# A comparison of two ways to transpose, put behind the last product of a Mamba-style layer and its feed-forward net

## The reference, cut to what matters

```python
x = x + _L0_attn_ref(_layernorm(x), ...)   # state-space layer: 128 heads of 64, 8 groups, gated, normed
x = x + _L0_ffn_ref(_layernorm(x), ...)    # gated feed-forward net, 1376 wide, with rank-16 additions
return x
```

```python
h1 = _lora_linear(x, w1, lora_A1, lora_B1)
h3 = _lora_linear(x, w3, lora_A3, lora_B3)
g = jax.nn.silu(h1) * h3
return _lora_linear(g, w2, lora_A2, lora_B2)
```

## Time and profile before

| | before |
|---|---|
| median of 3 executions | 1797.84 us (1797.22 to 1798.07) |
| the profiled execution, its own time | 1797.56 us |
| its span, first to last instruction | 1795.7 us |
| TensorE busy | 1762.8 us, 98% |
| VectorE busy | 1208.1 us, 67% |
| mean granted TensorE clock | 0.999 |

### The profile page before, as it was taken

The page is one execution under the profiler, slowest core; times in us unless marked ns, Lnnn a source line. Parts: engine busy times, 40 slices in busy tenths (PEclk is TensorE's granted clock), DMA queues, the critical chain, the costliest instruction groups (busy, mean ns, idle before and its releaser), DMA issues.

```text
span 1795.7 us, 27437 instructions
## 1 busy us (share of the span) xinstructions
PE 1762.8 (98%) x9826; PEld 1418.2 (79%) x9826; DVE 1208.1 (67%) x2081; ACT 1152.7 (64%) x2192; POOL 1079.3 (60%) x1011
## 2 busy tenths in 40 slices
PE   7999999999999999999999999999999999999999
PEld 5778887878788887888788878888788888787777
DVE  7796677757685768676876777576857697653313
ACT  5877577766766677667675776667666777552411
POOL 4475657566666567665756576666666575663510
PEclk9999999999999999999999999999999999999999
DMA  4643435333544443433534353345434443433201
GB/s 151 182 119 113 119 111 168 86 121 115 157 119 115 117 145 108 120 106 116 165 108 119 101 161 107 110 124 156 118 110 113 135 122 111 117 88 113 79 10 47
DMA packets 121878, 211.01 MB, mean 118 GB/s; under 512 B 24240, under 2 KB 28976, under 8 KB 121744
## 3 DMA queue, kind: packets, MB, share of 16 engines
q1 hardware_dynamic: 121744, 209.26, 40.3%
HBM read 204.48 MB, written 4.72 MB: 117 GB/s over the span
## 4 chain that ended last, share of the span: by engine, by line
PE 80%; DVE 8%; POOL 4%; issue 3%; DMA 3%; ACT 1%; SPq 0%; POOLq 0%; DVEq 0%; ACTq 0%
PE bank L1581 13%; PE bank L1583 13%; PE bank L1582 13%; PE bank L1692 6%; PE bank L1693 6%; PE bank L1694 6%; PE bank L1650 6%; PE bank L1680 5%; PE bank L1663 4%; DVE ow_l L1299 3%; DMA decay<-cum_scratch 3%; POOL gT_l L681 2%; PE bank L1626 2%; POOL decay L663 2%; PE bank L1901 1%
## 5 line engine op out<-in xcount | busy, mean ns | idle before, releaser
L657 POOL TENSOR_TENSOR w_l<-w_raw,w_h 128x512 fp32r<-128x512 f32 x288 | 380.2, 1324 | 465.2 <-ACT w_h L831 464.9
L1581 PE MATMUL bank<-x_h,w_h 128*128 128x512 f32 (+1 forms) x1328 | 532.9, 401 | 5.7 <-DVE bcT L1293 2.9
L1583 PE MATMUL bank<-x_h,w_l 128*128 128x512 f32 (+1 forms) x1328 | 519.1, 391 | 0.0
L1582 PE MATMUL bank<-x_l,w_h 128*128 128x512 f32 (+1 forms) x1328 | 518.1, 390 | 0.0
L1293 DVE SCALAR_TENSOR_TENSOR x_ch<-bank,par,x_ch 128x511 f32<-128x511 f32 (+2 forms) x384 | 287.5, 749 | 102.7 <-ACT x_ch L849 93.6
L884 ACT ACTIVATE decay<-decay,cols 128x128 f32<-128x128 f32 x1024 | 316.3, 391 | 0.8
L1581 PEld LDWEIGHTS bank<-x_h,w_h 128*128 128x128 f32 (+1 forms) x1328 | 249.3, 188 | 66.0 <-issue 8.7
L1583 PEld LDWEIGHTS bank<-x_h,w_l 128*128 128x128 f32 (+1 forms) x1328 | 248.8, 187 | 55.0
L1582 PEld LDWEIGHTS bank<-x_l,w_h 128*128 128x128 f32 (+1 forms) x1328 | 249.6, 188 | 48.0
L849 ACT ACTIVATE x_ch<-bank,par 128x512 f32<-128x512 f32 x128 | 99.4, 776 | 219.1 <-PE bank L1583 219.0
L1322 DVE TENSOR_TENSOR decay<-decay,bank 128x512 f32<-128x512 f32 x256 | 172.3, 682 | 92.9 <-ACT decay L884 92.7
(11 more groups left out here) (147 smaller groups left out, 2575.4 us busy)
## 6 DMA issues: line engine op xcount, KB each, us to landing
w_raw<-in_wp SPq DMA_DIRECT2D x288, 256.0 KB, 2.9
decay<-cum_scratch SPq DMA_DIRECT2D x256, 256.0 KB, 3.9
ec<-ecum_scratch SPq DMA_DIRECT2D x96, 256.0 KB, 6.4
ow_raw<-in_ow SPq DMA_DIRECT2D x64, 256.0 KB, 4.9
w_raw<-in_w SPq DMA_DIRECT2D x48, 256.0 KB, 2.7
acc<-in_x SPq DMA_DIRECT2D x8, 256.0 KB, 5.4
out<-acc SPq DMA_DIRECT2D x8, 256.0 KB, 2.0
cols<-cols_scratch SPq DMA_DIRECT2D x16, 96.0 KB, 2.8
```

The costliest lines, as they stand in the source:

```text
L657: pool.tensor_tensor(w_l[:, s, :], w_raw[:, s, :], w_h[:, s, :].bitcast(F32), ALU.subtract).then_inc(wl_ready, 1)
L1581: pe.matmul(dst, wh, xh, start=(k == 0), stop=False)
L1582: pe.matmul(dst, wh, xl, start=False, stop=False)
L1583: last = pe.matmul(dst, wl, xh, start=False, stop=(k == len(terms) - 1 and not more))
```

## The change

`acc` gets a second name, `acc_r`, of type fp32r at the same place in SBUF, and bank 1 gets the name `other` in that type. Two semaphores are new. TensorE gets eight transposes behind its last product: it waits until the results of chunks 0 and 1 are out of banks 0 and 1, then turns the four 128x128 tiles of chunk 7 of `acc` with fp32 operands into bank 0, and the same tiles with fp32r operands into bank 1, the two kinds in turn. VectorE waits for them after the addition of chunk 6, copies bank 0 to `xn`, subtracts bank 1, adds chunk 7's product to `acc` as before, and then adds 1e12 times the difference; only this last step increments `result_ready` for chunk 7.

```diff
-        acc = sb("acc", [P, CHUNKS, HID])
+        with nc.sbuf_tensor("acc", [P, CHUNKS, HID], F32) as acc:
+            pass
+        acc_r = sb("acc_r", [P, CHUNKS, HID], F32R)
...
+        other = bank[1].bitcast(F32R)
...
+        turned = sem("turned")
+        differ = sem("differ")
...
-            for c in range(CHUNKS):
+            for c in range(CHUNKS - 1):
                 dve.wait_ge(f_psum, c + 1)
                 dve.tensor_tensor(acc[:, c, :], bank[c][:, :], acc[:, c, :], ALU.add).then_inc(result_ready, 1)
+            dve.wait_ge(turned, 1)
+            dve.tensor_copy(xn[:, 0, :], bank[0][:, :]).then_inc(differ, 1)
+            dve.wait_ge(differ, 1)
+            dve.tensor_tensor(xn[:, 1, :], xn[:, 0, :], bank[1][:, :], ALU.subtract).then_inc(differ, 1)
+            dve.wait_ge(f_psum, CHUNKS)
+            dve.tensor_tensor(acc[:, CHUNKS - 1, :], bank[CHUNKS - 1][:, :], acc[:, CHUNKS - 1, :], ALU.add).then_inc(differ, 1)
+            dve.wait_ge(differ, 3)
+            dve.scalar_tensor_tensor(out=acc[:, CHUNKS - 1, :], in0=xn[:, 1, :], scalar=1e12, in1=acc[:, CHUNKS - 1, :],
+                                     op0=ALU.mult, op1=ALU.add).then_inc(result_ready, 1)
...
+            pe.wait_ge(result_ready, 2)
+            for q in range(KT):
+                pe.transpose(bank[0][:, tok(q)], acc[:, CHUNKS - 1, tok(q)], ident[:, :])
+                last = pe.transpose(other[:, tok(q)], acc_r[:, CHUNKS - 1, tok(q)], ident_r[:, :])
+            last.then_inc(turned, 1)
```

## The result

| | before | changed |
|---|---|---|
| median of 13 executions each | 1798.07 us (1797.10 to 1799.44) | 1801.74 us (1799.99 to 1802.11) |
| ratio to before, 95% interval | | 1.0018 (1.0009 to 1.0026) |
| span of the profiled execution | 1795.7 us | 1799.9 us |
| its own time | 1797.56 us | 1801.75 us |

The change costs 0.18%, about 3.2 us, with an interval from 1.6 to 4.7. That is inside the 0.2% that was called the same, as forecast, and near its edge: the interval reaches beyond it. The measured median lies 1.0 us above the predicted 1800.7 and inside the range.

A forecast was written before the change was run, and what follows sets the result against it. The prediction took the serial line from TensorE's last product to the last byte stored as the bound. TensorE's 0.77 plus VectorE's 2.05 gave 2.82 us on the 1797.84 us median, forecast 1800.7 us, range 1799.5 to 1802.3.

The forecast's parts named there:

- What bounds the end: Behind TensorE's last product, everything stands in series to the last byte stored; every added step costs its full length.
- VectorE's part: Copy, subtraction, addition and last operation at the end: 2.74 us where the addition alone took 0.69, 2.05 us added.
- TensorE's part: Eight transposes behind the last product, first start 0.23 us after it, each kind at its own step: 0.77 us added.
- The store: Chunk 7's store at the end: same size and place, 2.4 us from issue to end, only later.
- The sum: Steps added behind the last product: 0.77 + 2.05 = 2.82 us.
- The total: Time of the whole changed kernel: 1800.7 us, from the 1797.84 us median of three runs plus the added steps.
- this sign of being wrong: Ahead of the tail: the forecast would be wrong if TensorE's last product itself moved by more than 0.5 us.
- Rival 1: Between fp32 and fp32r transposes: alternation holds TensorE up, 1.2 us more, 1801.9 us (1803.0 with weight loads exposed); 17%.
- Rival 2: Under the eight transposes: the clock falls to 1.2 GHz, 0.8 us over forecast, 1801.5 us; 4%.
- Rival 3: Nearly nothing seen: steps overlap more, 1800.3 us, or an unrelated build difference; 3% for a gain over 3.6 us.

The follow-up runs named there:

- The parts alone: Two kernels: the changed kernel without VectorE's copy, subtraction and addition of the difference, 1799.56 us; the changed kernel without the eight transposes, 1800.56 us.
- the second: Profile of the changed kernel measured once more with no edit: 1801.57 us against 1798.43 for the kernel before, ratio 1.0015.
- the run with VectorE's part alone: The changed kernel without its eight transposes, the copy waiting for chunk 7's last product: 1800.56 us against 1798.43 for the kernel before, ratio 1.0012.

## Why the prediction was right

- What bounds the end: right. The parts alone (0.72 and 2.07 us behind the last product) add up to the whole (2.76 and 2.85). Moved out of the line, VectorE's part vanishes and TensorE's (0.78) stays, as TensorE is busy throughout.
- TensorE's part: forecast 0.77, measured 0.69. The start 0.23 behind the last product was right. The steps taken from each kind's own group were a little too long, since a pair in turn takes 0.17 and not 0.19.
- VectorE's part: forecast 2.05, measured 2.05. Each row read for it held: 0.69 for the copy, 0.72 from start to start with a wait, 0.60 to 0.61 without, 0.69 for the last operation.
- The store: forecast unchanged, 2.4 us; it was 2.43 in the first profile and 2.5 in the second, the same within the rounding of the span.
- The sum: forecast 2.82, and 2.76 in the first profile (2.85 in the second). The measured ratios, 1.0018 and 1.0015, are 3.2 and 2.7 us, with intervals that hold the sum.
- The total, 1800.7 against 1801.74: the total was 1.0 us off, and the steps behind the last product account for none of it. Of it 0.2 is the base: the median of three runs, 1797.84, stood for a kernel whose medians in the later sets were 1798.07, 1798.43 and 1798.98. The other 0.8 is what the medians of the first comparison differ by (3.67) beyond the forecast sum (2.82). It lies inside the interval (1.6 to 4.7), so it is not shown to be anything but spread. Everything ahead of the last product was forecast to stay "as it was", and by more than 0.5 us it did not; but neither does it in the unchanged kernel. So this sign of being wrong came up (1.44 us), and it was badly chosen: it asked of one profile what one program doesn't keep from one execution to the next. Over the profiles with the same stream ahead of the last product, that product starts anywhere from 1792.06 to 1794.26. The forecast had put the spread into its range by the 0.85 us between three runs, and it is over 3 us between 33. That the result counts as the same is in part luck: the interval reaches from 0.09% to 0.26%, across the line at 0.2%.
- Rival 1 (kinds in turn hold TensorE up): out; in turn is the faster order. Rival 2 (clock): out, also over 5.5 us. Rival 3 (a difference that has nothing to do with the steps): the medians are 3.67 and 3.14 us apart against the 2.8 of the tail, 0.3 to 0.9 more. The intervals hold 2.8, so such a difference is neither shown nor excluded.

The part ahead varies by 2 us in three places that the traces show: when the step between products gets shorter near the start, how long TensorE waits for GpSimd at 464 us, and what happens around the stretch of low clock near 1536 us (in the run with VectorE's part alone it lasted longer). What decides these from one execution to the next stays open.

## What to carry to other kernels

Work added behind the last product costs its full length, however short the engines' busy time makes it look. The same work where its engine sits idle is free: here that held for VectorE's part, not for TensorE's, and the banks for the comparison were free 11 us earlier. To price it, count from the last shared instruction in both traces and not from the start of the span: here the tail repeats to within 0.1 us while everything ahead of it moves by 2. On VectorE, a wait for its own last result costs 0.12 to 0.13 us for a 128x512 operation on fp32, so independent operations are best put between dependent ones.

## What was not expected of the hardware

- A transpose of a 128x128 tile took 0.109 us from start to start with fp32 operands and 0.084 with fp32r ones, but a pair in turn 0.174 rather than 0.193, over 28 pairs. The row of an fp32r transpose behind an fp32 one starts only 0.03 us behind it and lasts 0.31 instead of 0.25: such a row is long and early at once, and its length is no loss.
- One unchanged kernel of 1.8 ms spread over 3.4 us in 33 executions of one set, so three of them do not fix a base to within 0.5 us.
